# Unread bf16 products ahead of TensorE's waits in a four-layer kernel

## The chip, the core and the metric

The program runs on one core of a Trainium2 chip. The metric is the device time of one execution in microseconds; before the change three runs took 5806.01, 5807.99 and 5813.88 us, median 5807.99. Engines: TensorE (PE; its weight loads are PEld), VectorE (DVE), ScalarE (ACT), GpSimd (POOL) and SyncE (SP), which issues the DMAs.

## What is computed

The input is eight sequences of 512 rows with 128 features, all in float32. Each goes through four pairs of layers, every layer on the layer-normed input and added to it:

```python
x = x + L0_attn(norm(x))   # Mamba, forward and backward, 256 channels x 16 states
x = x + L0_ffn(norm(x))    # 16 experts of 64, grouped top-2 gate, and shared experts
x = x + L1_attn(norm(x))   # 16 heads of 64, bias by relative position
x = x + L1_ffn(norm(x))    # dense + 8 gated low-rank experts of rank 16
x = x + L2_attn(norm(x))   # 16 heads of 8, rotary positions, causal mask
x = x + L2_ffn(norm(x))    # own block: rotary attention without mask, then 8 experts of 512 (gelu)
x = x + L3_attn(norm(x))   # 16 heads of 8, memory with retention (a scan in time)
x = x + L3_ffn(norm(x))    # 8 experts of 256 with low-rank parts folded in
```

## The kernel before

Everything of a sequence ("a batch") stays in SBUF, 512 rows as four tiles of 128 (NJ = 4); weights are loaded once. PSUM's eight banks of 128 x 512 float32 are PS[0] to PS[7]. A stage is a block of five instruction streams, one for each engine, tied by semaphores; at a block's end all engines wait for each other. Stages of a batch, in `layers`: `moe0` (L0_ffn), `attn1`, `lora1` (L1_ffn), `attn2` and `attn3` (the two rotary attentions with heads of 8), `slot`. A hardware loop runs seven batches, the eighth is written out behind it (its tiles have a z ahead of their names). Batch b's Mamba layer runs in the slot stage of batch b-1, beside the rest of batch b-1 (`last_layers`: norm ln1, experts x2, norms ln2 and ln3, memory, norm ln4, experts x3). There each engine's stream is merged by `in_turn` from generators: each `yield t` names a due time, and the piece with the least goes next, so the order on every engine is fixed when the program is made. The first batch's Mamba layer has a stage of its own, `first`.

What the change and the steps behind it touch:

- `clear_on_all` (L150 to L178): the last block of the stages init, first and slot; each engine clears a fifth of the semaphores, TensorE in L163; SyncE stores the batch first.
- `norm_tiles` (L188): a norm as a block of its own, ahead of moe0, attn1, lora1, attn2 and attn3: statistics on VectorE (L215 to L220), the root on POOL (L202), scaled rows (L226), four transposes on TensorE (L251) as each tile of rows comes, copies out by ScalarE (L259) and VectorE (L240). TensorE has nothing else in the block.
- `head8_attention` (L367): score steps for 16 heads in four groups of four. Step s has an S product (L426, 64 rows by 128 columns of weights, 512 moving columns, bf16), whose maximum VectorE takes (L553, or with a mask L550), and, LAG = 20 steps later, a T product of the same shape with the maximum folded in (also L426), whose exponential ScalarE takes (L524). Heads alternate between rows 0 to 63 and 64 to 127 of the array. S and T share a ring of six banks: `bank_free` waits for the maximum or exponential that has the bank. Every fourth step four float32 products with 32 columns each weigh the values (L485, two passes, so eight records). The first 16 steps also have the transposes of q and k (`turn`, four bf16 transposes, L436) with copies on ScalarE (L504). Once a group eight bf16 transposes (L463) bring in the maxima, which VectorE has split (L559, L562), and four (L497) turn the output. N = 64, so steps run from 0 to 83, with S in the first 64 and T in the last 64. With a mask, S and T span 128 to 512 columns and POOL zeroes the diagonal (L533).
- `norm_parts` (L590): the same norm as generators, for the slot stage; TensorE's transposes are L652.
- `experts_parts` (L960): for each of n tiles an up product (L1010), in x3 also a gate product (L1013), and four down products (L1000). In x3 VectorE multiplies (L1065), in order behind the arithmetic of the gate's top-2.
- `memory_parts`: projections of q, k and v (L1121), splitting into bf16 parts, groups of eight transposes (L1138), then eight scan groups.
- the stage `lora1`: gate products (L291), low-rank products (L1833), dense products (L1837), then a wait for the gated values, transposes (L1841) and last products (L1845).
- `rope_attention` (L1873): a block with four projections (L1903, 384 columns, float32 in two passes each), the rotation on VectorE (L1948 to L1967) and copies on ScalarE, then `head8_attention` in a block of its own.

The change's place in a score step is between these lines:

```python
bank_free(pe, (kind, i))
tile, rows = i % PER // GH, slice(HS * (i % 2), HS * (i % 2 + 1))
lo, hi = span(kind, i)
nc.tensor.matmul(bank(kind, i), left[rows, P * tile:P * (tile + 1)], right[rows, lo:hi],
                 start=True, stop=True).then_inc(sem, 1)
```

## Time and profile before

| | |
|---|---|
| median of three runs | 5807.99 us |
| the profiled execution's own time | 5812.37 us |
| its span, first to last instruction | 5810.6 us |
| TensorE busy, x20516 | 4485.7 us (77%) |
| TensorE weight loads | 2226.2 us (38%) |
| VectorE busy | 3772.0 us (65%) |
| ScalarE busy | 3064.0 us (53%) |
| GpSimd busy | 1140.3 us (20%) |
| mean granted clock of TensorE | 0.844 |

The granted clock is the share of TensorE's full clock that the profile shows as granted: 1.00 is 2.4 GHz, 0.50 is 1.2 GHz, and it is at one of the two at any time. A product's record spans from its start until its end, with the way through the array; records of products that follow each other overlap, so how fast TensorE streams is read from start to start, and a busy TensorE is not one at its peak. The batch that is read here runs from 936 to 1653 us, the second turn of the loop. "x" and a number behind a row of the timeline is how many records are merged in it. Behind a row in brackets stands how long the engine was idle before, and what ended that.

### The profile page before, as it was taken

To read this page: it belongs to the slowest core of one execution; us is meant where nothing else is said; L and a number is where in the kernel's file an instruction comes from. 1 tells how busy PE (TensorE), PEld (TensorE's weight loads), DVE (VectorE), ACT (ScalarE), POOL (GpSimd) and SP (SyncE) were. 2 spreads that over 40 slices of the span, in tenths; PEclk is the share of its full clock that TensorE was granted. 3 is DMA by queue.
4 is the path that set the end of the run, shared out by engine and by line. 5 is a ranking of instruction groups with operands and counts; after the bars stand their busy time and mean duration, and the time that the engine had idled before them with its cause. 6 is when DMAs were issued, how large, how long until landed. Compare 5 with 4: busy or idle time off the path is not lost. (4 is left out here: it accounts for less than half of the span.)

```text
span 5810.6 us, 67170 instructions
## 1 busy us (share of the span) xinstructions
PE 4485.7 (77%) x20516; PEld 2226.2 (38%) x20516; DVE 3772.0 (65%) x8877; ACT 3064.0 (53%) x5351; POOL 1140.3 (20%) x1356
## 2 busy tenths in 40 slices
PE   5786778877788777887778777788778877788777
PEld 2342434424344243442434324343243433444334
DVE  6756586565865658656686556865668555686554
ACT  3365645556455555555655556555565555555443
POOL 2401132011320123201231012310123111231100
PEclk8996989978898788987889878897789987899778
DMA  4210021100210002100121001210012100121000
GB/s 160 87 36 1 21 65 55 32 1 25 67 55 26 1 28 71 52 22 1 34 73 47 20 1 37 75 48 13 1 42 75 46 11 1 44 73 47 7 1 2
DMA packets 104076, 218.53 MB, mean 38 GB/s; under 512 B 11072, under 2 KB 19776, under 8 KB 103152
## 3 DMA queue, kind: packets, MB, share of 16 engines
q1 hardware_dynamic: 103680, 213.81, 11.6%
q8 instruction: 180, 2.95, 0.2%
q14 instruction: 216, 1.77, 0.1%
HBM read 211.08 MB, written 2.69 MB: 37 GB/s over the span
## 5 line engine op out<-in xcount | busy, mean ns | idle before, releaser
L859 POOL TENSOR_TENSOR slot_work<-slot_work,slot_c_all 128x512 f32<-128x512 f32 x448 | 570.2, 1273 | 1015.9 <-DVE slot_work L942 1015.0
L777 PE MATMUL BANKS<-slot_work,WF 128*128 128x512 f32 x896 | 530.5, 679 | 5.7 <-DVE slot_du L918 2.9
L524 ACT ACTIVATE attn_prob<-BANKS 128x512 f32<-128x512 f32 (+3 forms) x896 | 401.5, 532 | 122.5 <-PE BANKS L426 119.0
L1000 PEld LDWEIGHTS BANKS<-WF,slot_x_a 128*128 128x128 f32 x2688 | 359.3, 197 | 264.5 <-ACT slot_x_a L1040 133.5
L1000 PE MATMUL BANKS<-WF,slot_x_a 128*128 128x128 f32 x2688 | 373.3, 283 | 86.3 <-ACT slot_x_a L1040 86.3
L1010 PE MATMUL BANKS<-XT,WF 128*128 128x512 f32 x768 | 425.3, 639 | 2.6 <-ACT slot_comb_t L306 2.6
L769 PE MATMUL BANKS<-slot_bcs,WB 96*128 96x512 bf16 x448 | 189.1, 422 | 305.1 <-DVE slot_work L942 304.0
L202 POOL TENSOR_TENSOR rstd<-rstd,WF 128x4 f32<-128x4 f32 x40 | 40.3, 1007 | 1572.7 <-DVE rstd L220 1559.5
L1809 DVE CUSTOM_DVE_ANT_0 attn_biased<-BANKS,attn_toep 128x512 f32<-128x512 f32 x448 | 306.0, 684 | 51.9 <-PE BANKS L1707 46.6
L1788 ACT COPY attn_probt<-BANKS 128x512 f32<-128x512 f32 x448 | 261.0, 583 | 147.3 <-PE BANKS L1714 144.4
L426 PE MATMUL BANKS<-attn_parts_kT,attn_parts_qT 64*128 64x512 bf16 (+3 forms) x896 | 309.2, 437 | 33.6 <-ACT attn_parts_qT L504 20.7
L935 DVE TENSOR_TENSOR BANKS<-BANKS,slot_du 128x512 f32<-128x512 f32 x448 | 307.6, 687 | 36.0 <-PE BANKS L769 33.4
L942 DVE TENSOR_TENSOR_SCAN slot_work<-slot_decay,BANKS 128x512 f32<-128x512 f32 x273 | 329.7, 1208 | 0.0
L1780 ACT ACTIVATE attn_prob<-attn_biased,attn_nmax 128x512 f32<-128x512 f32 x448 | 326.9, 730 | 1.3 <-DVE attn_nmax L1809 1.2
L553 DVE TENSOR_REDUCE attn_nmax<-BANKS 128x1 f32<-128x512 f32 x448 | 282.0, 683 | 67.9 <-PE BANKS L426 65.6
L1714 PE MATMUL BANKS<-WF,attn_prob 128*128 128x128 f32 x1792 | 280.3, 281 | 7.6 <-ACT attn_probt L1788 4.3
L550 DVE CUSTOM_DVE_ANT_0 attn_masked<-BANKS,WF 128x128 f32<-128x128 f32 (+1 forms) x448 | 202.1, 489 | 127.4 <-PE BANKS L426 126.6
L1714 PEld LDWEIGHTS BANKS<-WF,attn_prob 128*128 128x128 f32 x1792 | 190.9, 140 | 243.9 <-DVE attn_prob L1816 157.0
L1707 PE MATMUL BANKS<-attn_qk 64*128 64x512 f32 x896 | 257.8, 653 | 4.7 <-ACT attn_qk L1762 4.7
L426 PE MATMUL BANKS<-attn_qm,attn_parts_kT 64*128 64x512 bf16 (+3 forms) x896 | 238.8, 394 | 17.1 <-ACT attn_qm L510 11.3
L1814 DVE RECIPROCAL attn_rden<-attn_den 128x1 f32<-128x1 f32 x448 | 72.1, 161 | 275.3 <-ACT attn_prob L1780 272.3
L485 PE MATMUL BANKS<-attn_prob,attn_vals 128*32 128x512 f32 (+3 forms) x1792 | 226.1, 580 | 16.9 <-ACT attn_prob L524 10.7
(674 smaller groups left out, 9464.7 us busy)
## 6 DMA issues: line engine op xcount, KB each, us to landing
slot_c_all<-c_rows SPq DMA_DIRECT2D x448, 256.0 KB, 3.1
attn_toep<-bias_line SPq DMA_DIRECT2D x112, 448.0 KB, 4.4
first_c_all<-c_rows SPq DMA_DIRECT2D x64, 256.0 KB, 3.1
WF<-in_wf SPq DMA_DIRECT2D x4, 1964.0 KB, 16.2
zattn_toep<-bias_line SPq DMA_DIRECT2D x16, 448.0 KB, 4.3
WF<-in_wf SPq DMA_DIRECT2D x3, 800.0 KB, 17.2
WF<-in_wf SPq DMA_DIRECT2D x3, 785.5 KB, 6.0
XIN<-in_x SPq DMA_DIRECT2D x8, 256.0 KB, 2.9
```

The source lines that it names most:

```text
L426: nc.tensor.matmul(bank(kind, i), left[rows, P * tile:P * (tile + 1)], right[rows, lo:hi], start=True, stop=True).then_inc(sem, 1)
L524: nc.scalar.activation(prob[:, i % PR, lo:hi], bank("T", i), ACT.Exp).then_inc(exped, 1)
L553: V.tensor_reduce(nmax[:, j, h:h + 1], bank("S", s), AX.X, ALU.max, negate=True).then_inc(maxed, 1)
L777: nc.tensor.matmul(SUM, ident, work[:, m % RW, :], start=(n == 0), stop=(n == NS - 1)).then_inc(acc, 1)
L859: nc.gpsimd.tensor_tensor(work[:, m % RW, :], work[:, m % RW, :], c_all[:, m % RC, :], ALU.mult).then_inc(rd, 1)
L935: V.tensor_tensor(DRIVE[s % 3], DRIVE[s % 3], du[:, d, t, :], ALU.mult).then_inc(drv, 1)
L942: V.tensor_tensor_scan(work[:, m % RW, :], decay[m % RD], DRIVE[m % 3], 0.0, ALU.mult, ALU.add).then_inc(scn, 1)
L1000: last = nc.tensor.matmul(DOWN[e % 2][:, j * D:(j + 1) * D], a1[:, i % 3, j * P:(j + 1) * P], w_down[:, i * D:(i + 1) * D], start=(t == 0 ...
L1010: last = nc.tensor.matmul(place("up", i), w_up[:, i * P:(i + 1) * P], XT[:, :], start=True, stop=True)
L1714: last = nc.tensor.transpose(bank[:, kt * P:(kt + 1) * P], prob[:, u % NP_, kt * P:(kt + 1) * P], ident)
L1780: nc.scalar.activation(prob[:, e % NP_, :], biased[:, e % NS_, :], ACT.Exp, bias=nmax[:, e:e + 1], scale=-1.0, accum_out=den[:, e:e + 1]). ...
L1809: V.tensor_tensor_reduce(biased[:, s % NS_, :], PS[s % NS_], toep[:, h % 4, c:c + SEQ], -1.0, BIG, ALU.add, ALU.min, nmax[:, s:s + 1]).the ...
```

## The change

A helper `idle_products(bank, n)` issues n bf16 products of 128 rows by 128 columns with 512 moving columns. Weights are the bf16 identity, the moving operand is one of its columns repeated 512 times, and the result goes to a bank of PSUM that nothing reads before it is written again. They have no semaphores of their own. They are put ahead of TensorE's waits: 4 ahead of the clearing of semaphores, 8 ahead of and 3 behind the transposes of `norm_tiles`, one ahead of each S product and of the last 20 T products, 10, 20 and 8 ahead of the transposes of ln1, ln3 and ln4 (due one unit of the order before the norm), 12 in x3 between the third up and the third gate product, 16 ahead of memory's first transposes, 12 in lora1 ahead of the wait for gated values, and 40 behind the projections of a rotary stage. Nothing is removed, and no other engine's stream changes.

```diff
--- before.py
+++ after.py
@@ -159,6 +159,7 @@
 
         @block.tensor
         def _(pe):
+            idle_products(PS[3], 4)
             for s in sems[1::5]:
                 pe.sem_clear(s)
 
@@ -184,6 +185,11 @@
 
     def bc(ap, shape):
         return ap.to_broadcast(shape)
+
+    def idle_products(bank, n):
+
+        for _ in range(n):
+            nc.tensor.matmul(bank, ident_b, bc(ident_b[:, 0:1], [P, SEQ]), start=True, stop=True)
 
     def norm_tiles(st, tag, src, dst, dst_t, rms=False, gain_t=None, gain=None, shift=None, extra=None,
                    transposed=True, beside=lambda sp: None):
@@ -245,10 +251,12 @@
             if transposed:
                 @block.tensor
                 def _(pe):
+                    idle_products(PS[5], 8)
                     for j in range(NJ):
                         pe.wait_ge(normed, j + 1)
                         bank = PS[7] if j * P < HALF else PS[6]
                         nc.tensor.transpose(bank[:, j * P:(j + 1) * P], dst[:, j, :], ident).then_inc(turned, 1)
+                    idle_products(PS[5], 3)
 
                 @block.scalar
                 def _(act):
@@ -421,6 +429,7 @@
                 def score(kind, i, left, right, sem):
 
                     bank_free(pe, (kind, i))
+                    idle_products(PS[slot[kind, i]], int(kind == "S" or i >= N - LAG))
                     tile, rows = i % PER // GH, slice(HS * (i % 2), HS * (i % 2 + 1))
                     lo, hi = span(kind, i)
                     nc.tensor.matmul(bank(kind, i), left[rows, P * tile:P * (tile + 1)], right[rows, lo:hi],
@@ -588,7 +597,7 @@
             due[i] = next(streams[i], None)
 
     def norm_parts(st, tag, src, dst, small, at, dst_t=None, banks=None, rms=False, sq=None, gain_t=None, gain=None,
-                   shift=None, after=None):
+                   shift=None, after=None, spare=None, idle=0):
 
         s_stats, s_mv, s_rstd = small
         ch, normed, turned = st.sem(f"{tag}_chain"), st.sem(f"{tag}_normed"), st.sem(f"{tag}_turned")
@@ -645,6 +654,9 @@
         def tensor(pe):
             if dst_t is None:
                 return
+            if idle:
+                yield at - 1.0
+                idle_products(spare, idle)
             yield at + 3.6
             for j in range(NJ):
                 pe.wait_ge(normed, j + 1)
@@ -1010,6 +1022,8 @@
                 last = nc.tensor.matmul(place("up", i), w_up[:, i * P:(i + 1) * P], XT[:, :], start=True, stop=True)
                 if both:
                     last.then_inc(hid, 1)
+                    if i == 2:
+                        idle_products(DOWN[1], 12)
                     last = nc.tensor.matmul(place("gate", i), w_gate[:, i * P:(i + 1) * P], XT[:, :], start=True, stop=True)
                 last.then_inc(hid, 1)
                 if i >= 1:
@@ -1126,6 +1140,7 @@
                     yield at + 8.0 + 1.5 * k
                     if k == 0:
                         pe.wait_ge(cp, NJ)
+                        idle_products(PS[7], 16)
                     if i == 1:
                         pe.wait_ge(kn, 1)
                     else:
@@ -1276,7 +1291,8 @@
 
         SMALL = (stats, mv, rstd)
         Y = st.sb("Y", [P, NJ, D])
-        ln1 = norm_parts(st, "ln1", XN, Y, SMALL, 0.0, dst_t=XT, banks=(PS[5], PS[4]), gain=W("g1"), shift=W("be1_2"))
+        ln1 = norm_parts(st, "ln1", XN, Y, SMALL, 0.0, dst_t=XT, banks=(PS[5], PS[4]), gain=W("g1"), shift=W("be1_2"),
+                         spare=PS[7], idle=10)
         comb2, comb2_t = st.sb("comb2", [P, NJ, E2]), st.sb("comb2_t", [E2, SEQ])
         comb3, comb3_t = comb2, comb2_t
         shared = ExitStack()
@@ -1286,11 +1302,12 @@
             moe2 = experts_parts(box, "x2", gate2, ln1.ready, W("W1_2"), None, W("b1_2"), None, W("W2_2"), W("b2_2", E2), E2,
                                  FF // P, comb2, comb2_t, Y, 7.4, 2.0)
         ln2 = norm_parts(st, "ln2", Y, XN, SMALL, 73.0, gain=W("g2"), shift=W("be2_2"))
-        ln3 = norm_parts(st, "ln3", XO, XN, SMALL, 79.0, dst_t=XT, banks=(PS[5], PS[4]), after=(freed, 1))
+        ln3 = norm_parts(st, "ln3", XO, XN, SMALL, 79.0, dst_t=XT, banks=(PS[5], PS[4]), after=(freed, 1), spare=PS[4], idle=20)
         shared = ExitStack()
         with shared:
             memo = memory_parts(Box(st, shared), ln3.ready, XO, Y, 84.0)
-        ln4 = norm_parts(st, "ln4", XO, XN, SMALL, 132.0, dst_t=XT, banks=(PS[5], PS[4]), after=(memo.added, 1))
+        ln4 = norm_parts(st, "ln4", XO, XN, SMALL, 132.0, dst_t=XT, banks=(PS[5], PS[4]), after=(memo.added, 1),
+                         spare=PS[7], idle=8)
         shared = ExitStack()
         with shared:
             box = Box(st, shared)
@@ -1836,6 +1853,7 @@
                     for j in range(NJ):
                         nc.tensor.matmul(PS[2][:, j * P:(j + 1) * P], XT[:, j * P:(j + 1) * P], W("W_T"),
                                          start=(j == 0), stop=False, skip_group_check=True)
+                    idle_products(PS[3], 12)
                     pe.wait_ge(gated, 1)
                     for j in range(NJ):
                         last = nc.tensor.transpose(PS[1][:, j * P:(j + 1) * P], gh[:, j, :], ident)
@@ -1902,6 +1920,7 @@
                     for j in range(NJ):
                         nc.tensor.matmul(PS[j][:, 0:3 * D], XT[:, j * P:(j + 1) * P], w_qkv,
                                          start=True, stop=True).then_inc(pj, 1)
+                    idle_products(PS[5], 40)
 
                 @block.scalar
                 def _(act):
```

## Rows read from the trace of the kernel before

**Rows 1.** The page: span, and the strip of granted clock in 40 slices.

```profile
span 5810.6 us, 67170 instructions
...
PEclk8996989978898788987889878897789987899778
```

**Rows 2.** Busy time by stretch: us, PE, PEld, DVE, ACT, POOL (instructions), granted clock, DMA, GB/s.

```profile
936.00:953.20 17.20, 8.87 (x19) 4.96 (x20) 7.82 (x38) 4.46 (x6) 2.21 (x3) 0.50 0.02 6
...
1154.60:1188.70 34.10, 22.97 (x123) 9.76 (x124) 21.31 (x78) 18.22 (x34) 2.82 (x10) 0.50 0.00 1
...
1191.30:1202.30 11.00, 8.64 (x76) 3.27 (x76) 8.63 (x41) 7.32 (x18) 4.57 (x16) 1.00 0.01 1
...
1246.70:1280.90 34.20, 23.99 (x116) 9.47 (x116) 25.87 (x47) 17.94 (x31) 0.00 (x0) 0.50 0.00 1
...
1287.50:1299.60 12.10, 11.22 (x81) 3.33 (x77) 11.27 (x24) 9.89 (x20) 0.00 (x0) 1.00 0.00 0
```

**Rows 3.** Timeline (start us, us, engine, line), relative attention's projections at its start.

```profile
985.78 3.75 PE L1678 MATMUL BANKS<-XT,WF 128*128 128x512 f32 x4 [0.76 <-PEq L196]
...
995.27 1.12 PE L1678 MATMUL BANKS<-XT,WF 128*128 128x512 f32 x2
```

**Rows 4.** Timeline, score steps of the unmasked layer, high clock.

```profile
1287.52 0.39 PE L426 MATMUL BANKS<-attn_parts_kT,attn_parts_qT 64*128 64x512 bf16 x2
...
1287.74 0.38 PE L426 MATMUL BANKS<-attn_qm,attn_parts_kT 64*128 64x512 bf16 x2
...
1288.69 0.39 PE L426 MATMUL BANKS<-attn_parts_kT,attn_parts_qT 64*128 64x512 bf16 x1
...
1288.92 0.38 PE L426 MATMUL BANKS<-attn_qm,attn_parts_kT 64*128 64x512 bf16 x1
...
1289.22 1.06 PE L485 MATMUL BANKS<-attn_prob,attn_vals 128*32 128x512 f32 x8
...
1290.22 0.39 PE L426 MATMUL BANKS<-attn_parts_kT,attn_parts_qT 64*128 64x512 bf16 x2
```

**Rows 5.** One line's instructions: maxima (L553) and exponentials (L524), first and last start.

```profile
L553 DVE TENSOR_REDUCE attn_nmax<-BANKS x64: 677/680/694, 1256.8 to 1307.6; 128x1 f32<-128x512 f32 x64
...
L524 ACT ACTIVATE attn_prob<-BANKS x64: 591/603/716, 1276.1 to 1320.3; 128x512 f32<-128x512 f32 x64
```

**Rows 6.** Timeline, first score steps of the unmasked layer, low clock.

```profile
1262.16 0.60 PE L426 MATMUL BANKS<-attn_parts_kT,attn_parts_qT 64*128 64x512 bf16 x1
...
1262.70 0.61 PE L436 MATMUL BANKS<-WB,attn_parts_q 128*128 128x128 bf16 x4
...
1263.24 0.60 PE L426 MATMUL BANKS<-attn_parts_kT,attn_parts_qT 64*128 64x512 bf16 x1
```

**Rows 7.** Timeline, rotary stage of the unmasked layer.

```profile
1237.80 5.46 PE L1903 MATMUL BANKS<-WF,XT 128*128 128x384 f32 x8 [0.76 <-PEq L196]
...
1253.70 0.43 DVE L1962 CAST attn_parts_k<-attn_rot 128x512 bf16<-128x512 f32 x1
...
1254.43 0.59 PE L436 MATMUL BANKS<-WB,attn_parts_k 128*128 128x128 bf16 x4 [11.17 <-PEq L1886]
```

**Rows 8.** Timeline, transposes of two norms: at the loop's head and between layers.

```profile
940.55 0.87 DVE L215 BATCH_NORM_STATS2 stats<-X 128x6 f32<-128x128 f32 x4 [6.93 <-issue]
...
943.56 1.24 PE L251 MATMUL BANKS<-WF,XN 128*128 128x128 f32 x4 [10.67 <-DVE XN L226]
...
1235.80 1.24 PE L251 MATMUL BANKS<-WF,XN 128*128 128x128 f32 x4 [4.05 <-DVE XN L226]
```

**Rows 9.** Timeline, low-rank layer: gate products and last products.

```profile
1129.10 1.85 PE L291 MATMUL BANKS<-WF,XT 128*128 128x8 f32 x8 [0.76 <-PEq L196]
...
1138.09 2.08 PE L1845 MATMUL BANKS<-WF,lora_gh_t 128*128 128x128 f32 x8 [0.68 <-ACT lora_gh_t L1870]
```

**Rows 10.** Timeline, slot stage: memory's first transposes, and the third gate.

```profile
1469.33 1.06 PE L1138 MATMUL BANKS<-WB,slot_parts 128*96 128x128 bf16 x8 [0.42 <-ACT slot_parts L1186]
...
1565.72 0.75 DVE L1065 SCALAR_TENSOR_TENSOR slot_x_a<-BANKS,WF,slot_x_s 128x512 f32<-128x512 f32 x1 [2.68 <-PE BANKS L1013]
```

## The prediction

> **What bounds the kernel now.** I read the page first: its span of 5810.6 us, and in the strip of granted clock no slice at full and several near seven tenths [rows 1]. Then I cut one batch (936 to 1653 us, one turn of the loop) into stretches by the granted clock. The reader is to see two sorts of stretch in them [rows 2]. At 0.50, which is 1.2 GHz, run the start of a batch (936 to 953) and the first 34 us of both head-of-8 attention layers, there with TensorE busy two thirds of the time. At 1.00, which is 2.4 GHz, run the middles of the long stages. So no single engine bounds a batch: between stages it is the chain norm, transposes, products, in the score steps VectorE's maxima, in the expert stages TensorE and ScalarE in turn. The low clock costs time only where TensorE is on that chain. There are eight batches: seven through the loop and one written out behind it.
>
> **The price of one unread product.** A bf16 product of 512 columns streams in 0.22 us at the high level (start to start, 1287.52 to 1287.74) [rows 4]; twice that, 0.43, at the low one. I take the same for the new products; no row has a moving operand that repeats one column, so between 0.22 and, if that read were slow, twice it; I take 0.22, the nearest row.
>
> **Score steps, the large term.** There are 64 S and 64 T products per layer, four heads to a group, T 20 steps behind S. A new full-array product goes ahead of each S, and ahead of the last 20 T. In the layer without a mask, four steps take 2.70 us now, 1287.52 to 1290.22 [rows 4]. See how they come to it. Two S products start as a pair (x2, within one entry of 0.39 us): S and T use 64 rows of the array, and products on different halves run side by side. Then TensorE waits until 1288.69 for VectorE's maximum to free a bank. Then the four weighing products come, 1.00 us. A product over all 128 rows between them ends the pairing and fills the wait. It also brings changes between 64 and 128 rows, and such a change costs: 1288.92 (T, 0.23 behind the S at 1288.69) to 1289.22 is 0.30 where streaming takes 0.22; weighing to the next S is 1.00 where its two passes take 0.86; at the low level S to transposes and back are 0.54 each where 0.43 is streamed [rows 6]. That is 0.08 to 0.14 for a change; I take 0.10. After: 12 products x 0.216 = 2.6, 8 changes x 0.10 = 0.8, weighing 0.86, together 4.25 us. TensorE becomes the bound, VectorE's four maxima need some 2.4 us of it. So +1.55 for four steps, and 44 steps have S and T both: 11 x 1.55 = **+17.0 us**. Bounds: without any charge for the changes 3.45 to 3.7, +0.75 to +1.0 (8 to 11 us); with 0.14 each +1.9 (21 us).
> The tail of 20 T steps: from the last maximum to the last exponential 12.7 us now, 1307.6 to 1320.3 [rows 5]; after it 20 x (0.43 + 0.20) + 4 x 0.86 + 0.6 for transposes = 16.6, **+3.9**.
> The first 16 steps have an S and four transposes each, 1.08 us for a step, at the low level [rows 6]. The new product adds 0.43 there if the clock stays low; if it is high, a step is 3 x 0.22 + 2 x 0.10 = 0.86, that is 0.22 less. I take half the twelve later steps at either level, +1.2, and +0.5 for the first four with what follows before T begins: **+1.7**. This layer: +22.6.
> The causal layer has S and T of 128 to 512 columns but new products of 512 always. Sixteen steps take 11.0 us now, with TensorE busy 8.64 [rows 2]. After: S and T each 5120 columns, 2 x 2.16; weighing 2.15; products 16 x 0.216 = 3.45; 32 changes, 3.2; two sets of transposes 1.0: 14.1, so +3.1 for 16 steps and 8.5 for 44. The first twelve of those run at the low clock today and win 1.5 back; the tail's 20 products with their changes are 8.3 us, most of it in waits for exponentials and for POOL's mask, I take +2.5; start +1.5. **+11.0**, bounds +2 (all changes hidden) to +16. Both layers: **+33.6 us a batch**.
>
> **What the warm clock gives.** The four projections of a rotary stage take 5.46 us, almost all at the low level [rows 7]; at the high one about 2.8, and the rotary chain on VectorE starts that much sooner: -2.6 in each of two layers. The 40 products behind them are 8.6 us against 11.2 us until the first transpose at 1254.43, whose cover is VectorE's chain to 1253.70 [rows 7]; they cost nothing at the high level, and 6 us were they to run wholly at the low one. They leave 2.6 us open, so I expect the clock to be low again early in the score steps. Relative attention: four passes of its first projections are 3.75 us at the low level, two are 1.12 at the high one [rows 3]; with the following S and the next projection -3.4. The low-rank layer: its gate products take 1.85 at the low level and its last product 2.08 [rows 9]; -0.9 surely, the second only if twelve products keep the clock, -1.4 together. First experts: -1.4, an estimate: the 0.9 of eight such gate passes and a little of the first hidden products, since VectorE's gate chain is next. Transposes of five norms: -1.0. Together **-12.4**; bounds -4 and -20.
>
> **What the rest costs.** Eight products ahead of a norm's transposes are 3.4 us at the low level, 1.7 at the high. Between layers TensorE waits 4.05 us there and the wait covers them; at the loop's head the norm begins at 940.55 and the first transpose runs at 943.56 [rows 8], so they end about 0.9 late: **+0.9**. The three behind the transposes hold the end of the block: 0.65 against 0.45 us of copying, **+1.0** for five norms (+3 at the low level). The four ahead of the clearing of semaphores: **+0.4**, bounds 0 and 1.7. Slot stage, where TensorE also serves the scan of the next batch: ahead of memory's first transposes at 1469.33 [rows 10] sixteen products are 3.5 to 6.9 us, but these have slack, +0.6; ahead of the third gate's third product VectorE already waits 2.68 us for L1013 [rows 10], and twelve products lie straight on it, 12 x 0.216 = +2.6; norms there -0.4. **+2.8**.
>
> **Sum.** 33.6 - 12.4 + 0.9 + 1.0 + 0.4 + 2.8 = +26.3 us a batch; eight, 210. The last batch has no scan beside it, and its slot stage wins 3 rather than losing 2.8: 204. The profiled execution took 5812.4 us, 1.8 more than its span and 4.4 more than the median of 5808.0: 6016 on its scale, about **6010 us** as a median, 3.5% slower.
>
> **Rivals.** (a) *The changes between 64 and 128 rows are hidden*: 88 in the 44 steps of a layer, 40 in its tail, at 0.10 us some 12 us less there and 3 less in the causal layer, so +11 a batch and about 5895. For it: the gaps could be waits of another sort; against: they show at both clocks and at every such place. Chance 0.14.
> (b) *Faster.* The products stand only in time in which TensorE waits for VectorE: four score steps stay under 2.9 us, from there it decides. Then attention loses 1 us a batch, and gains 5 in its first steps at the high clock: -12.4 + 5.1 - 5 + 1 = about -9 to -11, 5725 to 5740. For it: VectorE's maxima do end a wait in rows 4; against: the wait is 0.3 us and four products are 0.86; I give it much because the pairing is read from few records. Chance 0.24.
> (c) *The first steps stay at the low clock.* That stretch, half of it bf16 transposes, is at 0.50 with 24 of 34 us busy [rows 2]. If those never help, sixteen steps lose 0.43 each in both layers: some 4 us more a layer, 8 x 8 = 64, so 6075. The Trainium skill, TensorE: Matmul & The Clock Gate, "Part 4: PE-mode transpose", says just this, that transposes don't count as busy for the clock; the trace agrees as far as it goes. By it the new time would be this one. Chance 0.10.
> (d) *The change does not do what it says*: unread products of one repeated column do not raise the clock. All costs stay and the gains go: +40 a batch and the 40 products late by 6 us twice, over 6150. Chance 0.03. (e) Gains and costs cancel, within 0.2%: 0.05.
>
> **Chances.** Forecast (5940 to 6060) 0.44, the rest above. Bounds of terms and cases (a), (c) and (e) alone would leave out over 2 in 10, so the range takes in most of (b) too: 5730 to 6110; the likeliest case alone has 5940 to 6060. A measurement here tells 0.2% (12 us) from no change. From the cases, (e) shared out at its edges: faster 0.25, same 0.04, slower 0.71.
>
> **What would show it.** Right: in steady score steps four take over 4 us with no wait on L553 and each S alone, not paired; VectorE idles there; L1903 takes under 3.5 us; L1013's reader waits over 4 us; granted clock well over 0.844. Wrong: four steps under 3 us, or S still in pairs; a clock no higher; L436 later than before because the 40 products overrun.

## The result and the profile after

The changed kernel takes 6248.83 us (median of four runs, 6232.63 to 6252.51), 1.0752 times the kernel before (95% interval 1.0731 to 1.0773). The forecast was 6010 with a range of 5730 to 6110: right in sign, short by more than half of the loss, and outside the range. The profiled execution's span is 6250.1 us, 439.5 more than before. Now and then an execution falls into a slower state; the runs' times below are medians without such ones (one of a4_short, 6481 us, and two of d3_no_slot, 6312 and 10707 us).

The page: span, then the strip of granted clock in 40 slices; it answers to [rows 1].

```profile
span 6250.1 us, 73338 instructions
...
PEclk8998989889899898988889988999899998999989
```

The clock is higher (0.898 against 0.844), as intended, and the kernel slower. Where the time went is read by taking the start of each stage from the timeline and adding up all eight batches. A score layer is counted from its first S to the first of its last output transposes, a rotary stage from its first projection to the first S.

| stage, eight batches | forecast, us | measured, us |
|---|---|---|
| score steps, unmasked layer | +181 | +321.7 |
| score steps, causal layer | +88 | +139.3 |
| rotary stages, two layers | -42 | -33.9 |
| relative attention | -27 | -23.4 |
| low-rank layer | -11 | -8.9 |
| first experts | -11 | +25.8 |
| slot stage, norms, the rest | +27 | +18.9 |
| sum | +205 | +439.5 |

The forecast column is the prediction's terms times eight, the last batch's slot stage allowed for. Two entries are far off: the score steps (461 us against 269), and the first experts, where the sign is wrong. The batch read below is again the second turn of the loop, now 989 to 1768 us.

Busy time by stretch of the changed kernel (columns as in [rows 2]): the unmasked layer, from the fall of the clock to its rise, and from there to the end.

```profile
1326.80:1371.10 44.30, 42.87 (x137) 12.03 (x137) 20.22 (x33) 14.53 (x25) 0.00 (x0) 0.50 0.00 1
1371.10:1433.40 62.30, 61.59 (x305) 16.21 (x304) 29.30 (x57) 38.16 (x63) 0.00 (x0) 1.00 0.00 1
```

Before, the low stretch was 34.2 us with TensorE busy 24 of them; now it is 44.3 us with TensorE busy 42.87. TensorE had been at the high level through the 40 products ahead, and fell as the score steps began. The average of before hides something. Cut at the first S (1256.18 us), its low stretch is two different things:

```profile
1246.70:1256.20 9.50, 1.03 (x10) 0.80 (x10) 7.05 (x14) 4.58 (x8) 0.00 (x0) 0.50 0.01 3
1256.20:1280.90 24.70, 22.96 (x108) 8.68 (x108) 18.81 (x33) 13.36 (x23) 0.00 (x0) 0.50 0.00 1
```

Most of the idle time stands ahead of the first S, under VectorE's chain. In the score steps themselves TensorE was busy 22.96 of 24.70 us, and the clock was low already. So a TensorE that is hardly ever idle can still be granted the low clock. The rows of before showed it; the forecast's main case did not draw on it, and only rival (c), with a chance of 0.10, allowed for it.

The first score steps at the low level (timeline: start, duration, engine, line); L445 is L436 of before, L435 is L426, L192 is the new product.

```profile
1335.63 0.61 PE L435 MATMUL BANKS<-attn_parts_kT,attn_parts_qT 64*128 64x512 bf16 x1
1336.17 0.61 PE L445 MATMUL BANKS<-WB,attn_parts_q 128*128 128x128 bf16 x4
1336.57 0.63 PE L192 MATMUL BANKS<-WB 128*128 128x512 bf16 x1
1337.14 0.61 PE L435 MATMUL BANKS<-attn_parts_kT,attn_parts_qT 64*128 64x512 bf16 x1
```

A step is 1.51 us (1335.63 to 1337.14) against 1.08 before [rows 6], 0.43 more, and no row shows the engine idle. Where S goes on to transposes of 128 rows, or a new product on to S, 0.54 to 0.57 us pass for 0.43 streamed, so 0.11 to 0.14 for a change; transposes to the new product, both of 128 rows, are 0.40. A step has two changes between 64 and 128 rows, as many as before: the new product stands beside the transposes, which have 128 rows too.

The steady steps at the high level, weighing (L494) to weighing, answering to [rows 4]:

```profile
1379.43 1.06 PE L494 MATMUL BANKS<-attn_prob,attn_vals 128*32 128x512 f32 x8
1380.43 0.39 PE L192 MATMUL BANKS<-WB 128*128 128x512 bf16 x1
1380.75 0.39 PE L435 MATMUL BANKS<-attn_parts_kT,attn_parts_qT 64*128 64x512 bf16 x1
1380.98 0.38 PE L435 MATMUL BANKS<-attn_qm,attn_parts_kT 64*128 64x512 bf16 x1
1381.29 0.39 PE L192 MATMUL BANKS<-WB 128*128 128x512 bf16 x1
...
1383.85 0.64 PE L494 MATMUL BANKS<-attn_prob,attn_vals 128*32 128x512 f32 x4
```

Four steps are 4.42 us (1379.43 to 1383.85), forecast 4.25. New product to S 0.32, S to T 0.23, T to new product 0.31, for 0.22 streamed: 0.09 to 0.10 for a change, as read before. No S is paired and VectorE's maxima wait for TensorE. The steady part was right.

Maxima and exponentials of the layer, one line's instructions, as in [rows 5]:

```profile
L562 DVE TENSOR_REDUCE attn_nmax<-BANKS x64: 684/692/693, 1328.7 to 1411.9; 128x1 f32<-128x512 f32 x64
...
L533 ACT ACTIVATE attn_prob<-BANKS x64: 597/597/604, 1358.4 to 1430.8; 128x512 f32<-128x512 f32 x64
```

The starts of the maxima span 83.2 us (50.8 before), the tail from the last maximum to the last exponential is 18.9 us (12.7 before): +6.2 where +3.9 was forecast.

The rotary stage ahead of it, as in [rows 7]:

```profile
1311.95 2.82 PE L1921 MATMUL BANKS<-WF,XT 128*128 128x384 f32 x8 [0.30 <-PEq L202]
1314.61 8.87 PE L192 MATMUL BANKS<-WB 128*128 128x512 bf16 x40
1325.94 0.38 PE L445 MATMUL BANKS<-WB,attn_parts_k 128*128 128x128 bf16 x4 [2.46 <-PEq L1904]
```

Projections 2.82 us against 5.46, the 40 products at 0.22 each under VectorE's chain, and 2.46 us open behind them: all as forecast.

The first experts, ahead of the transposes of the split gates (L1558) and in the down products behind them (L1542):

```profile
1017.28 1.05 PE L1542 MATMUL BANKS<-WF,moe_g 128*128 128x128 f32 x8
1021.04 0.42 PE L1558 MATMUL BANKS<-WB,moe_cp 128*96 128x128 bf16 x4 [2.70 <-DVE moe_cp L1609]
...
1026.38 1.91 PE L1542 MATMUL BANKS<-WF,moe_g 128*128 128x128 f32 x8
```

TensorE, started at the high clock, is through its up products 2.2 us sooner (16.9 us against 19.1) and then waits 2.70 us for VectorE's gates, which it did not do before; behind the wait the clock is low from 1023.0 to 1029.8, where it was high before, and the down products take 1.91 us instead of 1.05.

### The profile page after: what moved, and what is told of

The parts are those of the page before. It is cut to its first block and busy times, and to the rows that moved or that the text cites. A ratio compares the mean times of both kernels' runs of the same rounds, so it can differ in the third digit from the quotient of the medians.

```text
span 6250.1 us, 73338 instructions
## 1 busy us (share of the span) xinstructions
PE 5375.6 (86%) x23604; PEld 2476.1 (40%) x23604; DVE 3838.7 (61%) x8877; ACT 3133.5 (50%) x5351; POOL 1142.9 (18%) x1356
## 5 line engine op out<-in xcount | busy, mean ns | idle before, releaser
L192 PE MATMUL BANKS<-WB 128*128 128x512 bf16 x3088 | 1060.8, 430 | 127.6 <-issue 36.7
L533 ACT ACTIVATE attn_prob<-BANKS 128x512 f32<-128x512 f32 (+3 forms) x896 | 459.4, 518 | 378.1 <-PE BANKS L435 370.0
L192 PEld LDWEIGHTS BANKS<-WB 128*128 128x128 bf16 x3088 | 320.1, 105 | 817.9 <-issue 426.6
L789 PE MATMUL BANKS<-slot_work,WF 128*128 128x512 f32 x896 | 509.9, 655 | 6.2 <-DVE slot_du L930 3.4
L562 DVE TENSOR_REDUCE attn_nmax<-BANKS 128x1 f32<-128x512 f32 x448 | 309.7, 691 | 277.0 <-PE BANKS L435 277.0
L435 PE MATMUL BANKS<-attn_parts_kT,attn_parts_qT 64*128 64x512 bf16 (+3 forms) x896 | 368.4, 411 | 0.0
L559 DVE CUSTOM_DVE_ANT_0 attn_masked<-BANKS,WF 128x128 f32<-128x128 f32 (+1 forms) x448 | 218.1, 491 | 214.0 <-PE BANKS L435 210.8
L435 PE MATMUL BANKS<-attn_qm,attn_parts_kT 64*128 64x512 bf16 (+3 forms) x896 | 324.8, 363 | 0.8 <-ACT attn_qm L519 0.8
```

The source lines that it names most:

```text
L192: nc.tensor.matmul(bank, ident_b, bc(ident_b[:, 0:1], [P, SEQ]), start=True, stop=True)
L533: nc.scalar.activation(prob[:, i % PR, lo:hi], bank("T", i), ACT.Exp).then_inc(exped, 1)
L562: V.tensor_reduce(nmax[:, j, h:h + 1], bank("S", s), AX.X, ALU.max, negate=True).then_inc(maxed, 1)
L789: nc.tensor.matmul(SUM, ident, work[:, m % RW, :], start=(n == 0), stop=(n == NS - 1)).then_inc(acc, 1)
```

## Experiments

A layer's length and its time at the low clock are means of the eight layers of the profiled execution, in us, read as in the table above.

| run | time, us | ratio to before, interval | unmasked, of it low | causal |
|---|---|---|---|---|
| before | 5808 | 1 | 66.6, 24.7 | 63.0 |
| the change | 6249 | 1.0752 [1.0731, 1.0773] | 106.8, 46.4 | 80.4 |
| a1_no_score | 5787 | 0.9954 [0.9937, 0.9970] | 66.8, 26.0 | 63.6 |
| a2_score_only | 6280 | 1.0793 [1.0770, 1.0815] | 105.6, 43.8 | 81.7 |
| a3_same_half | 5899 | 1.0145 [1.0128, 1.0162] | 76.0, 26.4 | 66.9 |
| a4_short | 6386 | 1.0952 [1.0911, 1.0994] | 112.8, 93.8 | 91.4 |
| b1_first20 | 5916 | 1.0174 [1.0152, 1.0196] | 76.5, 34.1 | 68.5 |
| b2_after20 | 6214 | 1.0711 [1.0689, 1.0734] | 97.2, 37.3 | 83.4 |
| b3_real_data | 6254 | 1.0753 [1.0731, 1.0775] | 106.3, 45.2 | 81.3 |
| d2_grouped | 5914 | 1.0178 [1.0163, 1.0194] | 74.2, 3.7 | 66.1 |
| b4_burst50 | 5745 | 0.9901 [0.9884, 0.9918] | 63.5, 13.2 | 58.4 |
| c1_moe_fill | 5736 | 0.9868 [0.9851, 0.9884] | 63.0, 11.1 | 60.1 |
| c2_no_third | 5720 | 0.9847 [0.9831, 0.9863] | 62.4, 9.0 | 59.6 |
| c3_half_first | 5791 | 0.9956 [0.9940, 0.9973] | 64.4, 7.7 | 63.9 |
| c4_rotary_only | 5775 | 0.9934 [0.9918, 0.9951] | 62.9, 12.4 | 60.5 |
| d3_no_slot | 5733 | 0.9865 [0.9847, 0.9884] | 62.0, 6.8 | 60.3 |
| d1_best | 5725 | 0.9843 [0.9830, 0.9857] | 63.0, 11.1 | 61.9 |

### Which part costs: a1 and a2

```diff
 # a1_no_score: the changed kernel
-                    idle_products(PS[slot[kind, i]], int(kind == "S" or i >= N - LAG))
 # a2_score_only: the kernel before, with the helper and this one call
+                    idle_products(PS[slot[kind, i]], int(kind == "S" or i >= N - LAG))
```

> The changed kernel without the products ahead of S and T in the score steps; the others stay. Theory A (the loss is that TensorE streams on the chain in the score steps): in the changed kernel the unmasked layer takes 38.7 us more from first S to last output transposes (105.3 against 66.6) and the causal one 14 to 25 more, together some 57 a batch, which is all of the 55 lost; so 6249 - 8 x 57 = about 5790, 5770 to 5810, that is 0.0 to 0.6% faster than before. The first S of the unmasked layer still comes 2.6 us sooner. Rival B (the score steps are slow because the 40 products ahead of them, and not those in them, changed when the clock falls): the layers stay over 75 us and the time over 5900.

> The kernel before with only the products ahead of S and T in the score steps. Theory A: 5808 + 454 = about 6260 (6220 to 6290), the unmasked layer 105 us from first S to last output transposes, four steady steps 4.6 us at the high clock. Rival B: under 6050, the low-clock stretch of the unmasked layer no longer than the 34 us of before. Whether the two lists of products add up is read too: this time plus that of a1_no_score minus the changed kernel should be 5808 within 25 us.

Both came as theory A had them: 5787 and 6280 (6220 to 6290 was expected). The score-step products are the whole loss, and more; the rest of the change is a gain of 0.46%. The two parts add up (6280 + 5787 - 6249 = 5818 against 5808). Rival B, that the 40 products ahead shifted the clock, falls: without them, in a2, the layer is as long.

### Streaming or changes of rows: a3, a4, b3, d2

```diff
 # a3_same_half: weights and moving operand from rows 0-63 or 64-127, those of the S or T behind
-                    idle_products(PS[slot[kind, i]], int(...))
+                    idle_products(PS[slot[kind, i]], int(...), slice(HS * (i % 2), HS * (i % 2 + 1)))
 # a4_short: 128 moving columns
-                    idle_products(PS[slot[kind, i]], int(...))
+                    idle_products(PS[slot[kind, i]], int(...), P)
 # b3_real_data: what S or T streams, on all 128 rows
-                    idle_products(PS[slot[kind, i]], int(...))
+                    if kind == "S" or i >= N - LAG:
+                        t = i % PER // GH
+                        nc.tensor.matmul(PS[slot[kind, i]], left[:, P * t:P * (t + 1)], right, start=True, stop=True)
 # d2_grouped: four at a time
-                    idle_products(PS[slot[kind, i]], int(...))
+                    idle_products(PS[slot[kind, i]], 4 * int((...) and i % GH == 0))
```

Here `int(...)` and `(...)` stand for the condition of the changed kernel.

> The changed kernel with the score-step products on the 64 rows that the S or T behind them uses, so that no change between 64 and 128 rows is left between them. Price of a change 0.10 us at the high level: four steady steps 12 x 0.216 + 0.86 + 0.2 = 3.65 us against 4.6, sixteen first steps 0.11 x 32 = 3.5 us less at the same clock. Theory C (what raises the clock is rows in use, not time in use): with half the rows idle the low stretch of 44 us in the unmasked layer gets longer, the whole layer may stay low, then four steps are 7.0 us and the time is over 6350. Rival D (time in use decides): the clock pattern stays and the time is about 6249 - 8 x (11 x 1.0 + 3.5 + 2 in this layer, about half of it in the causal one) = 6050.

> The changed kernel with 128 moving columns instead of 512 in the score-step products, so the changes between 64 and 128 rows stay and three quarters of the streaming go. If changes are priced at 0.10 us and streaming at 0.216 per 512 columns: four steady steps at the high clock 4.6 - 4 x 0.16 = 3.95 us; at the low clock sixteen first steps 0.32 x 16 = 5.1 us shorter than the 24.2 of the changed kernel. If it were the number of products that costs, whatever their length, four steps would stay at 4.6. Time by the first: 6249 - 8 x (about 13 + 8) = 6080, if the low stretches keep their length; longer by up to 100 where they grow because less is streamed.

Both missed every range. With the same number of products and columns on 64 rows the loss falls from 441 us to 91; with a quarter of the columns but all the changes it grows to 574 (6386 against 5812, the kernel before in the same series). Busy time by stretch, first of a4 (its whole unmasked layer), then of a3 (low stretch, and the rest):

```profile
1336.70:1462.70 126.00, 124.56 (x440) 32.17 (x439) 49.35 (x90) 52.29 (x86) 0.00 (x0) 0.50 0.00 0
```

```profile
1268.90:1292.80 23.90, 23.16 (x104) 7.98 (x102) 13.53 (x24) 8.52 (x15) 0.00 (x0) 0.50 0.00 1
1292.80:1344.10 51.30, 48.73 (x338) 14.43 (x334) 32.18 (x66) 39.17 (x72) 0.00 (x0) 1.00 0.00 1
```

In a4 TensorE is busy 124.56 of 126.00 us and the clock never rises in that layer (four of the eight unmasked layers are like it, in the other four the low stretch ends after 61 us and the layer takes 99). So the busy share does not decide, and rival D, by which the time in use does, falls. a3's steady steps on the timeline, weighing to weighing:

```profile
1311.26 1.07 PE L494 MATMUL BANKS<-attn_prob,attn_vals 128*32 128x512 f32 x8
1312.26 0.40 PE L192 MATMUL BANKS<-WB 64*128 64x512 bf16 x2
1312.48 0.39 PE L435 MATMUL BANKS<-attn_parts_kT,attn_parts_qT 64*128 64x512 bf16 x2
1312.70 0.39 PE L435 MATMUL BANKS<-attn_qm,attn_parts_kT 64*128 64x512 bf16 x2
...
1314.39 1.07 PE L494 MATMUL BANKS<-attn_prob,attn_vals 128*32 128x512 f32 x8
```

Four steps are 3.13 us, 0.43 more than before the change and 1.29 less than with it, since S, T and the new products run in pairs (x2) again; I had forecast three products in a row for a step and no pairs. The pairs also spoil the test of theory C. A pair has one product on rows 0 to 63 and one on rows 64 to 127, at the same time, so these steps did not leave half the rows idle. In the first 16 steps, where most products on 64 rows ran one by one, the clock was low, and it rose as the pairs began. Whether the rows in use matter is therefore not decided by a3.

> The changed kernel with score-step products that stream what S streams (128 rows of the transposed q or k, weights from the other) in place of one repeated column of the identity; same shapes, same places, the result unread as before. Theory E (shape and change of rows decide, not what is streamed or how it is addressed): time 6249 within 20, low stretches of the same length, start to start of the same 0.54 and 0.32 us. Rival H (a repeated column counts for less in what sets the clock, or streams at another speed): the low stretch of the unmasked layer, 44 to 54 us now, falls to 30 or less and the time to under 6150.

6254 us and the same low stretches: what is streamed, or that one column is repeated, makes no difference. Rival H falls.

> The changed kernel with the same 64 and 20 products of a layer in groups of four, ahead of every fourth S (and every fourth of the last T), so that the streamed columns stay and three of four places where rows change from 64 to 128 and back go, and three of four pairs come back. Theory S (changes hold the clock low and cost 0.10 to 0.11 us each): the low stretch of the unmasked layer is 30 us or less, four steady steps 2.7 - 0.3 + 0.86 + 0.1 = 3.4 us, the layer about 66.8 + 7 + 11 x 0.7 + 3 = 84, the causal one about 70, time 5787 + 8 x (17 + 7) = 5980 (5930 to 6040). Rival T (the added streaming alone, wherever it is): low stretch over 40 us, time over 6150.

5914 us. The products, their rows and their columns are those of the change; they only stand four together. Its stretches, and rows of its steady steps:

```profile
1270.60:1277.50 6.90, 6.16 (x25) 2.02 (x23) 3.27 (x5) 1.28 (x3) 0.00 (x0) 0.51 0.00 0
1277.50:1346.50 69.00, 65.14 (x409) 20.75 (x415) 42.31 (x85) 46.00 (x84) 0.00 (x0) 1.00 0.00 1
```

```profile
1320.57 1.06 PE L494 MATMUL BANKS<-attn_prob,attn_vals 128*32 128x512 f32 x8
1321.57 1.04 PE L192 MATMUL BANKS<-WB 128*128 128x512 bf16 x4
1322.54 0.39 PE L435 MATMUL BANKS<-attn_parts_kT,attn_parts_qT 64*128 64x512 bf16 x2
1322.77 0.38 PE L435 MATMUL BANKS<-attn_qm,attn_parts_kT 64*128 64x512 bf16 x2
```

The low stretch is 6.9 us where the scattered products had 44.3, and the pairs are back. Rival T, the added streaming wherever it stands, falls: scattered, the score-step products cost 461 us over a1_no_score, grouped they cost 127 (5914 against 5787), so 334 are the price of scattering them.

What about the scattering keeps the clock low is not shown. Theory S has it that it is the changes between 64 and 128 rows. Between the first T and the last S the counts fit it: 90 changes in the trace of the changed kernel, 28 in d2, 26 before. But in the first 16 steps they do not. There the products stand beside transposes of 128 rows, and the changes are 26 before, 32 with the change and 28 in d2; from the sixth S to the sixteenth they are 20 in all three. Still the clock of before and of the change stays low through them, and that of d2 rises at 1277.5 us, during the sixth S, behind its second group:

```profile
1274.29 1.89 PE L192 MATMUL BANKS<-WB 128*128 128x512 bf16 x4
1276.11 0.60 PE L435 MATMUL BANKS<-attn_parts_kT,attn_parts_qT 64*128 64x512 bf16 x1
1276.65 0.61 PE L445 MATMUL BANKS<-WB,attn_parts_k 128*128 128x128 bf16 x4
1277.19 0.53 PE L435 MATMUL BANKS<-attn_parts_kT,attn_parts_qT 64*128 64x512 bf16 x1
1277.65 0.40 PE L445 MATMUL BANKS<-WB,attn_parts_q 128*128 128x128 bf16 x4
```

What differs there is that four products of 128 rows stream in a row. And a4 has the same 90 changes as the change, and its clock stays low for far longer. So the number of changes alone does not explain it, and three readings are left: changes of rows, the ended pairs (which leave half the array's rows idle beside each S and T), and the lack of an unbroken run of products on all rows. In the steps with S and T all three go together in the change, a4 and b2, and all three are undone in d2; no run here parts them.

The Trainium skill, TensorEngine Tiling (Array Packing), "Key Properties", says that a change of tiling mode drains TensorE; the 0.09 to 0.14 us at each change of rows agree.

### Which steps: b1 and b2

```diff
 # b1_first20: ahead of the first 20 S only
+                    idle_products(PS[slot[kind, i]], int(kind == "S" and i < LAG))
 # b2_after20: not ahead of them
+                    idle_products(PS[slot[kind, i]], int(kind == "S" and i >= LAG or kind == "T" and i >= N - LAG))
```

> The changed kernel with the score-step products ahead of the first 20 S of a layer alone; none where T runs beside S. In a1_no_score the first 16 S of the unmasked layer take 15.5 us and the low stretch ends 24 us behind the first S; in the changed kernel 24.2 and 43. Theory E (the products of the first steps cost their own streaming and two changes and raise nothing; what keeps the clock low later are the changes among S, T and new products): 16 steps 24.2, low stretch ends 30 to 35 us behind the first S, when S and T have run paired for as long as before; layer 66.4 + 9 to 12 = about 77, causal layer 68 to 71, time 5787 + 8 x (11 + 7) = 5930 (5880 to 5960). Rival F (these products are what pays): the clock is high by the fourth group of transposes and the time is under 5800.

> The changed kernel without the score-step products ahead of the first 20 S of a layer; the rest stay. Theory E: first 16 S 15.4 us as without any; then 44 steps at 1.2 us (4.7 for four) where the clock is high and 2.0 (8 for four) where it is low, tail +4; if the clock rises 24 us behind the first S as before, the unmasked layer is 66.4 + 11 x 1.9 + 4 = 91, if the changes keep it low for another 15 us it is 100. Time 5787 + 8 x (25 to 34 and 12 to 18 in the causal layer) = 6080 to 6200, and the sum with b1_first20 is the changed kernel's loss: both over a1_no_score together 461 within 60. Rival G (the low first steps are what delays the rise, not the changes): the layer stays under 88 and the time under 6060.

b1's time and lengths came as theory E had them (the low stretch of the layer read here ends 30.7 us behind the first S, 24.4 without these products and 43.1 with all). b2 is 14 us over the range, and the two losses together are 556 us against 461: they do not add up. In four of the eight unmasked layers of b2 the low stretch ends 41.8 us behind the first S, in the other four 33 to 34, with the first 20 steps left as they were. So the scattered products beside S and T keep the clock low for longer by themselves, and in the change both parts lengthen the same stretch. Rival G falls.

### What the gain is made of: b4, c1 to c4, d1, d3

All but c4 build on a1_no_score.

```diff
 # b4_burst50: a1 and
-                    idle_products(PS[5], 40)
+                    idle_products(PS[5], 50)
 # c1_moe_fill: b4 and, in the first experts' stage,
+                    idle_products(PS[4], 12)
                     pe.wait_ge(parted, 1)
 # c2_no_third: b4 and
-                    if i == 2:
-                        idle_products(DOWN[1], 12)
 # c3_half_first: b4 and, on the rows of S,
+                    idle_products(PS[slot[kind, i]], int(kind == "S" and i < PER), rows)
 # c4_rotary_only: the kernel before and
+                    idle_products(PS[5], 50)
 # d3_no_slot: c2 and
-            idle_products(PS[3], 4)
-                idle_products(spare, idle)
-                        idle_products(PS[7], 16)
 # d1_best: c2 and the line of c1
```

> a1_no_score with 50 products behind the projections of a rotary stage in place of 40, so that TensorE streams up to the first transposes of the score layer (the 40 end 2.4 us ahead of them, 1323.5 to 1325.9 in the changed kernel; ten take 2.2 at the high level). Theory I (the clock falls some us into the first steps whatever stands ahead, since in them TensorE waits for ScalarE's copies): the low stretch of each layer starts 2 to 4 us later and ends no earlier, first 16 S 14 to 15.6 us, time 5770 to 5787. Rival J (the open 2.4 us is what lets it fall): the low stretch of 24 us goes, 16 S take about 11, time 5787 - 16 x 4 = 5723. If the ten come late instead, the first S is 0.5 or more later in both layers and the time over 5790.

5745 us, between the two theories: 42 us less than a1. The first 16 S take 9.7 (causal) and 11.6 us, against 13.6 and 15.5 in a1, and the low clock in the unmasked layer halves (13.2 us). With ten products more, which close the gap of 2.46 us to 0.30, the high level reaches into the first steps (in five unmasked layers it falls 14 us behind the first S, in three 3 us behind it).

> b4_burst50 with 12 more unread products in the first experts' stage, ahead of TensorE's wait for the split gates (the changed kernel waits 2.70 us there at 1018.3 to 1021.0, the kernel before did not, and its clock is low from 1023.0 to 1029.8). Theory K (the change made that wait and with it the low clock behind it: the stage is 3.3 us longer though its start is 2.5 us faster): 12 x 0.216 = 2.6 us fill the wait, the low stretch of 6.8 us goes, the stage falls from 43.7 to 39.5 (from 40.4 to 38.5 with all of it), time 5745 - 8 x 4.2 = 5712. Rival L (the wait is for VectorE and the clock would be low whatever TensorE does in it, or the 12 are late): stage 43 to 46, time 5740 to 5765.

```profile
956.97 1.05 PE L1541 MATMUL BANKS<-WF,moe_g 128*128 128x128 f32 x8
957.87 2.77 PE L192 MATMUL BANKS<-WB 128*128 128x512 bf16 x12
960.73 0.42 PE L1558 MATMUL BANKS<-WB,moe_cp 128*96 128x128 bf16 x4
```

The 12 products fill the wait and the low stretch behind it is gone: the stage falls from 43.5 to 40.7 us (means of eight batches), so theory K holds there. But the relative attention behind it then takes 141.3 to 141.6 us instead of 139.7 in six batches of eight, with a low stretch of its own (979.6 to 983.0 in this one), so only 9 of the 33 us expected are left. The intervals of c1 and b4 touch.

> b4_burst50 without the 12 products ahead of the third gate product of x3. In the changed kernel x3 starts 1.4 us sooner than before and its last up product comes 1.5 later: 3 us lost, forecast 2.6. Theory M (they lie straight on the path of VectorE's third multiplication): 8 x 2.9 = 23 us less, 5722. Rival N (x3 is at the high clock because of them): 5740 to 5760.

5720 us, 26 less than b4, as theory M had it: the 12 products lie on the path.

> b4_burst50 with one product on S's own 64 rows ahead of each of the first 16 S. In b4 the first 16 S take 9.7 (causal) and 11.6 us, part of it at the low level. Theory O (a step of S, four transposes and one more product is 3 x 0.216 and two changes at 0.10 = 0.86 us at the high level, over the 0.59 us copy that bounds it): if it keeps the clock high 16 S take 13.8, what follows gains 1 to 2, time 5745 + 16 x 1.5 = 5770; if it does not, 18 to 21 us and the time 5850. Rival P (it costs nothing, being beside the copy, and keeps the clock high through the layer): 5700 to 5730.

5791 us, 46 more than b4: products in the first steps cost more than they give even on S's own rows. The low time of the unmasked layer falls to 7.7 us and the layer is still longer; the first 16 S take 13.8 and 12.7 us.

> The kernel before with only the 50 products behind the projections of each rotary stage. Theory Q (what stands ahead of the projections matters: without the norm's products they run at the low level, 5.46 us, and so do the first of the 50, so that the 50 end some 3 us behind the 11.2 us that VectorE's chain leaves): first S 18 to 20 us behind the first projection, against 15.6; the first 16 S as short as in b4 (9.7 and 11.6); time 5808 - 8 x (4.4 + 3.3) + 16 x 0 to 2 = 5745 to 5780. Rival R (the 50 are all that pays, and the other products cost some 3 us a batch): 5808 - 8 x (2 x 2.5 + 4.5 + 3.2) = 5707, and under 5735.

5775 us, as theory Q had it, with the first S 18.1 us behind the first projection (15.6 in b4).

> c2_no_third without the products of the slot and first stages too (clearing, ln1, ln3, ln4, memory); left are those of the block norms, of the low-rank layer and 50 behind each rotary projection. In the changed kernel memory's first transposes come 4.5 us later than before and the scan groups behind them at the same time, so those products neither pay nor cost; the clearing costs 0.4. Theory U: time 5719 within 10. Rival V (ln4's and ln3's products raise the clock for x3's and memory's projections, worth 1.4 us a batch): 5725 to 5735.

5733 us; its interval overlaps that of c2, so whether the slot stage's products pay is unclear. No cost of theirs is seen.

> b4_burst50 with both edits: 12 products ahead of the first experts' wait for the split gates, none ahead of the third gate product. If the two gains add up, 5745 - 9 - 26 = 5710; the low stretch that the fill takes out of the first experts' stage came back in the relative attention in c1 (141.5 against 139.7 us), so 5705 to 5725.

5725 us, no better than c2_no_third (5720). c2 and d1 are 1.5 to 1.6% faster than the kernel before.

## Why the prediction failed, point by point

- **A product's price, a change's price, steady steps.** Right. 0.22 and 0.43 us for a product, 0.09 to 0.14 for a change, four steady steps 4.42 us against 4.25, and VectorE's wait for the third gate grew from 2.68 us to 6.28, as the signs of being right had it. Rival (a), that the changes are hidden, and rival (b), that the products only fill waits, are out by the timeline.
- **"I take half the twelve later steps at either level"** (with the first four steps and what follows, +1.7 us until T begins). This is the step that failed: the clock of the first steps. In the unmasked layer all of them ran at the low level, at 0.43 us more a step. The first T comes 29.7 us behind the first S instead of 19.3, +10.4 (means of eight layers): 16 x 0.43 = 6.9 for the first 16, and 3.5 more where S had run in pairs or in a row, at the start and in the last four steps ahead of T.
- **"44 steps have S and T both: 11 x 1.55"** (+17.0) took the high level for all of them. In the layer read here it came 43.1 us behind the first S instead of 24.7 (in three of the eight layers 52), 13 us into the steps with T, and there a step is 1.51 us of streaming and changes with no wait to hide in. From the first T to the last S the trace has 55.2 us instead of 31.0, +24.2; 11 x (4.42 - 2.70) = 18.9 of them are the steady price. Behind the last S it is +5.6 where +3.9 was forecast. Together the layer is 40.2 us longer, not 22.6. The causal layer (+17.4 for +11.0) errs the same way, +4.8 until T begins for +1.5: its two layers of 87.7 us were at the low clock for 37.5 us, its five of 76 to 78 for 9 to 14.
- **The reason behind both** was the belief that more products can only raise the clock. It rests on a reading of [rows 2] that averages too much. "The first 34 us of both head-of-8 attention layers, there with TensorE busy two thirds of the time" begin 9.5 us ahead of the first S. From the first S on TensorE was busy 22.96 of 24.70 us at the low level, so there was hardly any idle time for the new products to fill. Rival (c) doubted the rise for the first steps, for another cause (half of them transposes) and at some 4 us a layer (its own 16 x 0.43, less the +1.7 in the sum, gives 5.2). It had the direction. Its cause is not what the runs show: in d2 the same transposes stand between grouped products, and the clock rises 6 us in; and in the change the clock stays low for 13 us of steps with T, in which no transposes are left. The Trainium skill, TensorE: Matmul & The Clock Gate, "Part 4: PE-mode transpose", holds that transposes don't count; no run here tests that by itself. What it is in scattered products that keeps the clock low stays open, as said under d2_grouped.
- **Warm gains.** Rotary stages, relative attention and low-rank layer gave 66 of 80 us forecast. The first experts were "-1.4, an estimate": +3.2 a batch, by the wait of 2.70 us and the low clock behind it.
- **The slot stage.** The third gate's 12 products cost 26 us in all (2.6 a batch forecast, 3.3 measured). Slot stage, norms and the rest were 2.4 us a batch together where 3.4 was forecast. That sum is right in part by luck, since the third gate alone took 0.7 more than its term.
- **Rival (d)** is out: where the products stand in a block, the clock rises.

## What to carry to other kernels

Here unread products bought clock as a block, under cover of a long wait, and joined to the work behind it: 50 behind each rotary projection gave 42 us more than 40, while one ahead of each S and of the last 20 T cost 461. Ahead of each added product ask how many rows the products before and behind it use: one of 128 rows between two of 64 ends their pair and costs time at both changes, and so scattered it went here with a low clock. Before counting on idle time that a filler could use, cut a low stretch where the work changes: an average over two stages showed a third of idle time that the stage in question did not have. And where a warm start makes TensorE early for a wait that it did not have, look at the clock behind that wait.

## What the hardware showed that was not expected

TensorE at 124.56 us busy of 126.00 kept the low level throughout, with short products of all 128 rows (128 moving columns) scattered between products of 64 rows; with products of 512 columns in groups of four (d2) it was at the high level after 6.9 us. With new products of 64 rows (a3) the clock rose after 23.9 us, when S, T and they began to run in pairs on both halves. Layers of one kernel, with the same instructions, fell into groups by where the clock happened to change: in a4 four unmasked layers took 99 us and four 126.
